# Two attention layers on one core: image rows in runs of 128 tokens, x loaded ahead of the weights, bias vectors by TensorE

## The reference

```python
def layer(x, gamma, beta, wq, bq, wk, bk, wv, bv, wp, bp, eps):
    xn = group_norm(x, 32 groups of 8 channels, over all 1024 tokens, eps) * gamma + beta
    q, k, v = xn @ wq + bq, xn @ wk + bk, xn @ wv + bv
    attn = softmax(q @ k.T / sqrt(256))          # 1024 x 1024 for each image
    return (attn @ v) @ wp + bp + x
```

## Time and profile before

| | before |
|---|---|
| median of 3 runs | 274.82 us (274.56 to 275.66) |
| the profiled execution | 275.11 us, with a span of 273.3 us |
| mean granted TensorE clock | 1.000 |
| busy: TensorE, its weight loads | 95%, 85% of the span |
| busy: VectorE, ScalarE, GpSimd | 63%, 55%, 40% |
| DMA | 7.37 MB, nearly all input in the first 20 us |

### The profile page before, as it was taken

How to read it: one execution, slowest core, us unless ns; L and a number is a source line. 1 busy time by engine, 2 the same in 40 slices (tenths; PEclk the granted TensorE clock), 3 DMA queues, 4 the chain that set the end, 5 groups by cost and what they waited for, 6 DMA issues and landing times.

```text
span 273.3 us, 4591 instructions
## 1 busy us (share of the span) xinstructions
PE 258.9 (95%) x1650; PEld 233.5 (85%) x1650; DVE 172.9 (63%) x436; ACT 151.5 (55%) x295; POOL 110.5 (40%) x111
## 2 busy tenths in 40 slices
PE   3999899999979999999989999999999999999994
PEld 2788688889978899879988899879988899889993
DVE  0499576786685557475976557475976547554623
ACT  3465454499867607670686616680577506670650
POOL 2016200186444814461264723471064733550680
PEclk9999999999999999999999999999999999999999
DMA  5960000000000000000000000000110000100102
GB/s 169 329 235 1 0 1 2 0 0 2 0 1 2 1 2 0 0 1 2 0 1 2 0 2 0 0 0 2 40 41 0 1 22 19 38 2 19 48 12 77
DMA packets 5965, 7.37 MB, mean 27 GB/s; under 512 B 556, under 2 KB 4664, under 8 KB 5944
## 3 DMA queue, kind: packets, MB, share of 16 engines
q1 hardware_dynamic: 5920, 7.08, 7.7%
q10 hardware_dynamic: 24, 0.01, 0.0%
HBM read 4.99 MB, written 2.10 MB: 26 GB/s over the span
## 4 chain that ended last, share of the span: by engine, by line
PE 61%; DVE 20%; ACT 9%; issue 6%; POOL 1%; DMA 1%; DVEq 0%; ACTq 0%; POOLq 0%
PE ring L910 9%; PE ring L912 9%; PE ring L911 9%; PE O L949 6%; PE O L951 6%; PE O L950 6%; DVE S L641 4%; DVE xn_lo L570 3%; ACT S L400 3%; DVE xnat L651 2%; ACT P_hi L399 2%; DVE xraw L563 2%; DVE t_lo L606 2%; ACT S L392 2%; PE ring L896 2%
## 5 line engine op out<-in xcount | busy, mean ns | idle before, releaser
L285 POOL TENSOR_TENSOR P_lo<-S,P_hi 128x512 fp32r<-128x512 f32 x64 | 82.9, 1302 | 107.9 <-ACT S L400 107.9
L949 PE MATMUL O<-V,P_hi 128*128 128x258 f32 x208 | 59.9, 288 | 0.0
L951 PE MATMUL O<-V,P_lo 128*128 128x258 f32 x208 | 58.9, 283 | 0.0
L950 PE MATMUL O<-V,P_hi 128*128 128x256 f32 x208 | 58.8, 282 | 0.0
L392 ACT COPY S<-ring 128x512 f32<-128x512 f32 x64 | 37.5, 587 | 37.6 <-PE ring L912 34.8
L910 PE MATMUL ring<-t_hi,xn_lo 128*128 128x512 f32 x128 | 51.4, 402 | 0.8 <-DVE t_lo L606 0.8
L399 ACT ACTIVATE P_hi<-S 128x512 fp32r<-128x512 f32 x64 | 40.6, 635 | 19.8 <-DVE S L641 18.1
L912 PE MATMUL ring<-t_hi,xn_hi 128*128 128x512 f32 x128 | 50.1, 392 | 0.0
L911 PE MATMUL ring<-t_lo,xn_hi 128*128 128x512 f32 x128 | 50.0, 391 | 0.0
L624 DVE TENSOR_TENSOR R<-ring,R 128x512 f32<-128x512 f32 x48 | 33.0, 688 | 24.7 <-ACT S L392 24.0
L641 DVE TENSOR_TENSOR S<-X,S 128x512 f32<-128x512 f32 x64 | 42.3, 681 | 0.0
(11 more groups left out here) (114 smaller groups left out, 407.5 us busy)
## 6 DMA issues: line engine op xcount, KB each, us to landing
xnat<-in_x SPq DMA_DIRECT2D x8, 256.0 KB, 6.8
out<-xnat SPq DMA_DIRECT2D x16, 128.0 KB, 1.9
wide<-in_vectors SPq DMA_DIRECT2D x2, 384.0 KB, 7.2
w_wq<-in_L_conv_wq SPq DMA_DIRECT2D x2, 256.0 KB, 4.9
w_wk<-in_L_conv_wk SPq DMA_DIRECT2D x2, 256.0 KB, 5.0
w_wv<-in_L_conv_wv SPq DMA_DIRECT2D x2, 256.0 KB, 6.7
w_wp<-in_L_conv_wp SPq DMA_DIRECT2D x1, 256.0 KB, 6.8
w_wp<-in_L_conv_wo SPq DMA_DIRECT2D x1, 256.0 KB, 6.9
```

Source lines behind the costliest of these rows:

```text
L285: nc.gpsimd.tensor_tensor(P_lo[:, tile, :], S[:, tile, :], P_hi[:, tile, :].bitcast(F32), ALU.subtract).then_inc(po_P, 1)
L949: nc.tensor.matmul(bank[:, 0:C + 2], P_hi[:, tile, mine], v[:, kb, 0:C + 2], start=(kb == 0), stop=False)
L950: nc.tensor.matmul(bank[:, 0:C], P_hi[:, tile, mine], v[:, kb, C + 2:VX], start=False, stop=False)
L951: last = nc.tensor.matmul(bank[:, 0:C + 2], P_lo[:, tile, mine], v[:, kb, 0:C + 2], start=False, stop=(kb == NB - 1))
```

## The change

- A token tile k now holds tokens 128k to 128k + 127, so x and the output are read and written with partition stride of one row. A part of x (256 tokens) is now 256 runs of 1 KB out of one solid 256 KB.
- SP loads image 0 first, then the four weights of layer 0, the four of layer 1, bp of both layers (128 KB each, broadcast), then image 1. `wide` and `products` are gone.
- att comes from TensorE: behind the matmuls of an A product, two matmuls of one column multiply wkT by bq (column of vec_cols), and for mc = 1 two more multiply bk by bq. `A_high` gets one more activation, which scales them. `attention_vector` is gone.
- VectorE sets R[:, 0:128] to ones first, and TensorE starts with four matmuls of these ones, whose result in Z is not used (`keep_running`), and one more behind the transposes of wq.
- The parts of x go to ring banks 0 to 3; bn_stats of image 0 reads the banks directly, and ScalarE's copy waits for it.
- The order of the head is new on each engine. On TensorE: x, vectors, wq, wk, the group mean, wv, the variance, A_product(0), two weights of layer 1, Wx_product(0), the third weight, two t products, both output biases, two t products, A_product(1), Wx_product(1), scores.

```diff
-    x_rows = x.rearrange("b (p k) c -> b p k c", k=NB)
+    x_rows = x.rearrange("b (k p) c -> b p k c", k=NB)
     vectors_of_layer = vectors.rearrange("(a l v) c -> a l v c", a=1, v=NV)
-    out_rows = out.rearrange("b (p k) c -> b p k c", k=NB)
+    out_rows = out.rearrange("b (k p) c -> b p k c", k=NB)
...
-            def load_wide(l):
-                at = VECTORS.index(WIDE[0])
-                sp.dma_start(wide[:, l], vectors_of_layer[:, l, at:at + len(WIDE), :].to_broadcast([P, len(WIDE), C])
-                             ).then_inc(ld_wide[l], 16)
-
-            load_weights(0, ("wq", "wk"))
             load_image(0)
-            load_weights(0, ("wv", "wp"))
-            load_weights(1, ("wq", "wk"))
-            load_wide(0)
-            load_weights(1, ("wv", "wp"))
-            load_wide(1)
+            load_weights(0, ("wq", "wk", "wv", "wp"))
+            load_weights(1, ("wq", "wk", "wv", "wp"))
+            for l in range(LAYERS):
+                sp.dma_start(bp_rows[:, l], vectors_of_layer[:, l, VECTORS.index("bp"), :].to_broadcast([P, C])
+                             ).then_inc(ld_bp, 16)
             load_image(1)
...
                     act.wait_ge(dv_xl, v * TQ)
+                else:
+                    act.wait_ge(dv_bn, r + 1)
                 nc.scalar.copy(xraw[:, :, 2 * r * P:2 * (r + 1) * P], bank[:, :].rearrange("p (k n) -> p k n", k=KC)
...
                 nc.scalar.activation(A_hi[:, l, k, :], bank[:, 0:C], ACT.Identity, scale=SCALE)
+
+                cols = 1 if k < KC - 1 else 2
+                nc.scalar.activation(att[:, l, k:k + cols], bank[:, C + 1:C + 1 + cols], ACT.Identity, scale=SCALE)
                 nc.scalar.activation(Wx_hi[:, l, k, C:C + 1], bank[:, C:C + 1], ACT.Identity, scale=SCALE
...
-            weight_transposed(0, 0)
-            weight_transposed(0, 1)
             for r in range(NR):
-                raw_rows(0, r, ring[2 + r % 2])
-                if r == 2:
-                    A_high(0, 0)
-            A_high(0, 1)
-            weight_transposed(0, 2)
+                raw_rows(0, r, ring[r])
+            for n in range(3):
+                weight_transposed(0, n)
+            for k in range(KC):
+                A_high(0, k)
             weight_transposed(1, 0)
             weight_transposed(1, 1)
+            xn_high(0, 0)
+            xn_high(0, 1)
             for k in range(KC):
             weight_transposed(1, 2)
-            for q in range(TQ):
-                xn_high(0, q)
-            A_high(1, 0)
-            A_high(1, 1)
-            for k in range(KC):
-                Wx_high(1, k)
+            xn_high(0, 2)
+            xn_high(0, 3)
...
                     t_high(0, h, k)
+            for k in range(KC):
+                A_high(1, k)
+            for k in range(KC):
+                Wx_high(1, k)
             for kb in range(NB):
...
             def statistics_of(v, r):
-                dve.wait_ge(ac_xT, v * NR + r + 1)
+                if v:
+                    dve.wait_ge(ac_xT, v * NR + r + 1)
+                else:
+                    dve.wait_ge(pe_xT, r + 1)
                 for k in range(KC):
-                    last = nc.vector.bn_stats(bn[:, k, r, :], xraw[:, k, 2 * r * P:2 * (r + 1) * P])
+
+                    rows = xraw[:, k, 2 * r * P:2 * (r + 1) * P] if v else ring[r][:, 2 * k * P:2 * (k + 1) * P]
+                    last = nc.vector.bn_stats(bn[:, k, r, :], rows)
                 last.then_inc(dv_bn, 1)
...
                                   ).then_inc(dv_vec, 1)
-            statistics_of(0, 0)
-            statistics_of(0, 1)
-            statistics_of(0, 2)
+            for r in range(NR):
+                statistics_of(0, r)
+            channel_statistics(0)
+            group_deviation(0)
+            variance(0)
+            affine_map(0)
+            normalise(0, range(0, 2))
             A_low(0, 0)
-            statistics_of(0, 3)
-            channel_statistics(0)
+            xn_low(0, 0)
             A_low(0, 1)
-            attention_vector(0, 0)
-            group_deviation(0)
...
-                Wx_low(1, k)
+            xn_low(0, 1)
+            normalise(0, range(2, 4))
+            for k in range(KC):
+                Wx_low(0, k)
+            xn_low(0, 2)
+            xn_low(0, 3)
...
-            for h in range(HALVES):
-                for k in range(KC):
-                    t_low(0, h, k)
+            for k in range(KC):
+                t_low(0, 0, k)
+            for l in range(LAYERS):
+                output_bias(l)
+            for k in range(KC):
+                t_low(0, 1, k)
+            for k in range(KC):
+                A_low(1, k)
+            for k in range(KC):
+                Wx_low(1, k)
             for kb in range(1, NB):
...
                 for kd in range(KC):
-                    last = nc.tensor.matmul(bank[:, 0:C + 1], wqT[:, l, kd, mc * P:(mc + 1) * P],
-                                            wkT_bk[:, l, kd, :], start=(kd == 0), stop=(kd == KC - 1))
+                    nc.tensor.matmul(bank[:, 0:C + 1], wqT[:, l, kd, mc * P:(mc + 1) * P],
+                                     wkT_bk[:, l, kd, :], start=(kd == 0), stop=(kd == KC - 1))
+                bq = l * NV + VECTORS.index("bq")
+                for kd in range(KC):
+                    last = nc.tensor.matmul(bank[:, C + 1:C + 2], wkT_bk[:, l, kd, mc * P:(mc + 1) * P],
+                                            vec_cols[:, kd, bq:bq + 1], start=(kd == 0), stop=(kd == KC - 1))
+                if mc == KC - 1:
+                    for kd in range(KC):
+                        last = nc.tensor.matmul(bank[:, C + 2:C + 3], wkT_bk[:, l, kd, C:C + 1].to_broadcast([P, P]),
+                                                vec_cols[:, kd, bq:bq + 1], start=(kd == 0), stop=(kd == KC - 1))
                 last.then_inc(pe_A, 1)
...
                 pe.wait_ge(ld_w[l, "wp"], 16)
-                if l == 0:
-                    pe.wait_ge(ac_xT, NR - KC + mc + 1)
                 bank = ring[2 + mc][:, 0:C] if l == 0 else X[:, mc * C:(mc + 1) * C]
...
+            def keep_running(n):
+
+                for _ in range(n):
+                    nc.tensor.matmul(Z[:, 0:P], R[:, 0:P], R[:, 0:P], start=True, stop=True)
+
+            pe.wait_ge(dv_ones, 1)
+            keep_running(4)
             pe.wait_ge(po_const, 5)
-            transpose_weight(0, 0)
-            pe.wait_ge(ld_vec, 16)
-            for k in range(KC):
-                last = nc.tensor.transpose(X[:, k * LAYERS * NV:(k + 1) * LAYERS * NV],
-                                           vec_rows[:, k * P:(k + 1) * P], ident[0:LAYERS * NV, 0:LAYERS * NV])
-            last.then_inc(pe_vec, 1)
-            transpose_weight(0, 1)
             for r in range(NR):
                 pe.wait_ge(ld_x[0][r], 16)
-                if r >= 2:
-                    pe.wait_ge(ac_xT, r - 1)
-                transpose_rows(ring[2 + r % 2], 0, r)
-                if r == 2:
-                    A_product(0, 0)
+                transpose_rows(ring[r], 0, r)
+                if r == 0:
+                    pe.wait_ge(ld_vec, 16)
+                    for k in range(KC):
+                        last = nc.tensor.transpose(X[:, k * LAYERS * NV:(k + 1) * LAYERS * NV],
+                                                   vec_rows[:, k * P:(k + 1) * P], ident[0:LAYERS * NV, 0:LAYERS * NV])
+                    last.then_inc(pe_vec, 1)
+            transpose_weight(0, 0)
+            keep_running(1)
+            transpose_weight(0, 1)
+            mean_of_groups(0)
+            transpose_weight(0, 2)
+            variance_of_groups(0)
+            A_product(0, 0)
             A_product(0, 1)
-            transpose_weight(0, 2)
             transpose_weight(1, 0)
             transpose_weight(1, 1)
-            mean_of_groups(0)
-            Wx_product(0, 0)
-            variance_of_groups(0)
-            Wx_product(0, 1)
+            for mc in range(KC):
+                Wx_product(0, mc)
             transpose_weight(1, 2)
-            pe.wait_ge(dv_stat, VARE)
-            for l in range(LAYERS):
...
-                Wx_product(1, mc)
...
                     pe.wait_ge(dv_xl, u * TQ + (h + 1) * KC)
+                if u == 0:
+
+                    if h == 0:
+                        pe.wait_ge(dv_A, KC)
+                    else:
+                        pe.wait_ge(dv_Wx, KC)
                 wait_for_bank("t", u, h, k)
...
-            for h in range(HALVES):
-                for k in range(KC):
-                    t_product(0, h, k)
+            for k in range(KC):
+                t_product(0, 0, k)
+            pe.wait_ge(dv_stat, VARE)
+            for l in range(LAYERS):
+                output_bias(l)
+            for k in range(KC):
+                t_product(0, 1, k)
+            for mc in range(KC):
+                A_product(1, mc)
+            for mc in range(KC):
+                Wx_product(1, mc)
             for kb in range(NB):
```

(31 more changed lines are left out.)

15 lines of the change are left out of this document (removed).

## The result

The changed kernel takes 276.49 us (median of 20 runs, 276.21 to 277.14) against 275.71 us for the kernel before in as many (274.56 to 276.16). The ratio is 1.0034, 95% interval 1.0024 to 1.0043: slower by 0.3%, 0.8 to 0.9 us. The three runs of before that stood ahead of the prediction are the first three of its twenty, and their median of 274.82 lies near the low end; so the level of my 275.3 is 1.2 too low, and the difference, forecast as +0.5, is +0.8 to +0.9. The profiled execution after takes 276.25 us with a span of 274.5, 1.2 above the span before.

A forecast was written before the change was run, and what follows sets the result against it. TensorE bounds the kernel and the first score matmul sets the end: x's fourth part at 6.8, plus 2.2 to the group mean, 8.3 to the first t product, 12.0 to scores, gives 29.3, +0.5: median 275.3 us, range 273.4 to 277.2.

The forecast's parts named there:

- What bounds the kernel: TensorE, busy 95% of 273.3 us; the head's first score matmul, at 28.81, sets the end one for one.
- S: Start of the first score matmul, 28.81 us in the kernel before; forecast at 29.3, 0.5 later.
- T to S, 12.0: TensorE, first t product to first score matmul: 12.0 us, including 1.2 for layer 1's six one-column matmuls at 0.20 each.
- M to T, 8.3: Start of the group mean to first t product: 8.3 us, set by ScalarE's queue, where xn_high(0,0) stands behind layer 1 weight copies.
- X3, 6.8: Landing of the fourth part of x: 6.8 us, nearer to landing by form, with half the third issue's delay.
- the third place: Third load in the queue: its issue took 0.95 us where the second took 0.46, a delay that may belong to place.
- M = X3 + 2.2: Group mean starts 2.2 us after x's fourth part lands: transposes 0.60, two bn_stats 0.75, ScalarE's copy 0.58, small waits.
- Rival 4: Ones end ahead of x, TensorE slow until about 11; group mean 9.6 to 10.1, +1.1 to +1.6 us; no separate chance.
- Rival 1: Loads land by queue place: fourth part of x at 8.4, first score matmul 30.9, +2.1 us; chance 0.25.
- The removed products: VectorE's layer 1 products open the queue ahead of t_lo; without them the 0.95 us from 27.86 to 28.81 goes.
- The number: Whole kernel: median 274.82 + 0.5 = 275.3 us; this case, within 1.4 us either way, has chance 0.55.

The follow-up runs named there:

- after again: The changed kernel run once more, unedited, against the kernel before on the same chip: ratio 1.0034.
- xn_high moved: Changed kernel with ScalarE's xn_high(0,0) and xn_high(0,1) right behind A_high(0,0) and A_high(0,1), ahead of layer 1's two weight copies: ratio 1.0003 to the kernel before.
- no ones: Changed kernel without any matmul of ones (both keep_running calls removed): ratio 1.0026 to the kernel before.
- early table: Changed kernel with a two-column copy ahead of ScalarE's first real copy, so its table loads in idle time at the start: ratio 1.0029 to the kernel before.

## Why the prediction was right, and where it was not

- *What bounds the kernel.* Right. A shift of S is a shift of the end, in all fourteen traces.
- *T to S, 12.0.* Measured 12.01 (18.16 to 30.17). The term I could not see in the trace, 0.20 for a one-column matmul, is 0.18 (0.22 with a broadcast column as weights): six are 1.17, not 1.2.
- *M to T, 8.3.* Measured 8.45 (9.71 to 18.16), and its cause, ScalarE's order, shown by moving it.
- *X3, 6.8.* Measured 6.5 and 7.2 in two executions of the changed kernel, 6.3 to 7.2 in all nine of its order and form. The issue of long duration that I had put down to the third place came in one of these two (0.93) and not in the other (0.46): it belongs to the execution.
- *M = X3 + 2.2.* This step failed. It would be 8.7 and 9.4 with the two measured X3; M is 9.71 both times. So the term is not only too small (3.2 and 2.5): the landing of the fourth part is not where the chain begins. In five of the nine traces (after, after again, xn_high moved with and without att of layer 1 by VectorE, no ones) M comes 5.85 us after TensorE's start on the first part of x, at 3.68 to 3.86, while X3 goes from 6.4 to 7.2; in the other four it comes right behind the transposes of wk, 5.86 to 6.49 after that start. The reason is work in sequence behind the first part. TensorE transposes at the lower rate and comes to the fourth part only at about 7.1 (an estimate: two thirds into the twelve that start at 5.19 and take 2.82), where I had set 0.60 for its transposes right at X3. And ScalarE's four copies follow one another from the end of the table load, which starts with the statistics of the first part, at 6.31. Left out of the sum was that load: it lay at 1.47 before, and I did not ask what hides it once the first copy also has to wait for bn_stats. By itself it is worth little: with the early table the last copy ends 5.62 after TensorE's start on x and not 5.81, now bound by bn_stats, and the transposes of wk then cover it. So I can't split the excess between the load and the slow transposes; that the copies hold the mean is shown where TensorE is ahead (waits of 0.68 without ones, 0.33 with xn_high moved, 0.19 in the repeat).
- *Rival 4*, the ones end too early and TensorE is slow up to the statistics, came true in its size (M 9.6 to 10.1), and its reason, the slow transposes, is part of what happened. Rival 1 did not come; its S of 30.9 was nearer to the result than the forecast's 29.3, for another reason.
- *The removed products.* The 0.95 us of waiting went as said. What I did not draw from it: that it goes as well by moving them, for nothing, while one-column matmuls pay 1.17 twice for it.
- *The number.* By the prediction's own measure S was forecast at 29.3, +0.5, and came at 30.17, +1.4. That the medians moved by only 0.8 to 0.9 comes in the main from the traced execution of before, 0.6 faster than its median; so the closeness of +0.5 to the measured difference is in part luck.

So the change is a gain and a larger loss. The layout gives 2.0 us (0.9928 in the old order). The new orders, the one-column matmuls and the ones together take 2.9 us net (0.9928 to 1.0034), and 3.2 in the old layout (1 to 1.0116); each of these differences is known to some 0.6 us. The net holds a second gain, the wait ahead of the first score matmul, worth 0.8 us on top of the new layout (0.9928 to 0.9900). Against the kernel that has both gains the changed one loses 3.7 us (0.9900 to 1.0034; 4.0 by S, 26.16 to 30.17). Of these the one-column matmuls of layer 1 are 1.3 to 1.5 us (S - T, and 0.0056 between the two runs with xn_high moved), ScalarE's order 0.85 to 1.2 us. The rest, 1.0 to 1.5 us, was not split further; layer 0's one-column matmuls take 1.2 us of TensorE ahead of T, beside the ones and the waits around the mean. The prediction had the sum right within 0.4 us and never saw the two parts, since it asked only for the break-even of the whole.

On the two rules: the Trainium skill, DMA: Bandwidth & Descriptors, Why small descriptors are slow, gives a fixed overhead to each packet, from which the prediction's estimate was that x in runs of 1 KB takes about 4% longer than in 2 KB. Here the parts in 1 KB runs landed first, the fourth at 6.3 to 7.2 against 8.3, so something else in the form outweighs it in this head, the solid block being the candidate. The measurement decides. The prediction also read that rule's sign out of 341 GB/s in 8 to 12 us against 405 in 14 to 17; that does not hold, since three parts of x in the 2 KB form landed in the first of these stretches (8.4, 9.1 and 9.9). In TensorE: Matmul & The Clock Gate, The HAM clock gate, of the Trainium skill, activity releases the throttle. The traces agree that the durations halve only after work; that the ones bring it forward is not shown: the first transposes at the higher level come at 7.67 with none, at 7.94 and 9.09 with four, among those from 5.13 with six.

## What to carry to other kernels

Where one moment of the head sets the end, sum the head backwards from it by queue, and ask of every wait that goes whether moving the work on the idle engine takes it too: three instructions moved gave 0.9 to 1.1 us, and the matmuls that replaced them cost more. A step that is moved ahead of others in an in-order queue should be followed by what is urgent, not by what is merely early: the two weight copies of layer 1 cost 0.85 to 1.2 us. A chain that starts with the last landing should be checked against the queue that starts with the first: here four parts in sequence set the mean, not the last of them. And price each part of a change by itself, since gains of nearly 3 us in it can hide a loss of nearly 4.

## What the runs showed of the hardware that I had not expected

- A 256 KB load taken as 2 KB at every 8 KB lands later than one taken as one solid block of 1 KB runs, when little else is in flight: 8.3 to 8.5 us in three traces against 6.3 to 7.3 in eleven, each time for the fourth load of the queue.
- ScalarE's table load (1.28 us) does not always run at the start: it ran at 1.47 in the kernel before, ahead of the one wait of a first copy that came at 4.87, and at 6.31 in the changed kernel, behind the two waits of its first copy; an early copy brings it back to 1.47. Whether the number of waits decides was not tried.
- A one-column float32 matmul with 128 x 128 weights costs TensorE 0.18 us, while one of 256 columns costs 0.43 (output_bias, four in 1.73 us): a 256th of the columns, and still over 40% of the time.
- VectorE's product over 256 columns takes 0.85 to 0.95 us in the two traces where GpSimd adds the residuals beside it, and 0.41 to 0.42 where it does not; eight of the residual adds take 6.15 us beside the products and 5.53 to 5.62 without.
- The moment when TensorE's durations halve moves by over 1 us between executions of one kernel (7.9 and 9.1 us), and the landing of the fourth load by 0.7 us (6.5 and 7.2).
